# A perceiver layer stack with windowed attention and a quantised feed-forward: the last gated columns rounded on GpSimd, and a new order from the end of the last layer on

## The reference

```python
x = x + xattn(layernorm(x), ctx, seg)   # 4 layers: self-attention, masked cross-attention, gated feed-forward; rmsnorm at the end
x = x + attn(layernorm(x))              # each token looks at the 16 before it: sigmoid(q k / 4) times v, Wo, layernorm
x = x + ffn(layernorm(x))               # quantised
```

```python
_weight_quant(w): scale = 1 / clip(mean(|w|), 1e-5);  clip(round(w * scale), -1, 1) / scale
_act_quant(x):    scale = 127 / clip(max(|x|, -1), 1e-5);  clip(round(x * scale), -128, 127) / scale
_bitlinear(x, w) = _act_quant(x) @ _weight_quant(w).T
out = _bitlinear(silu(_bitlinear(x, w_gate)) * _bitlinear(x, w_up), w_down)
```

## Time and profile before

| | |
|---|---|
| median of 3 runs | 622.28 us (620.0 to 622.4) |
| the profiled execution's own time | 619.67 us |
| its span, first to last instruction | 617.9 us |
| mean granted TensorE clock | 0.991 of full speed |
| busy: PE, DVE, ACT, POOL | 564.1, 353.5, 279.5, 117.7 us |
| split_low, L1903 | 64 instructions, 48.0 us, mean 755 ns |

### The profile page before, as it was taken

The page is one execution under the profiler, slowest core; times in us unless marked ns, Lnnn a source line. Parts: engine busy times, 40 slices in busy tenths (PEclk is TensorE's granted clock), DMA queues, the critical chain, the costliest instruction groups (busy, mean ns, idle before and its releaser), DMA issues.

```text
span 617.9 us, 13676 instructions
## 1 busy us (share of the span) xinstructions
PE 564.1 (91%) x5806; PEld 421.8 (68%) x5806; DVE 353.5 (57%) x680; ACT 279.5 (45%) x490; POOL 117.7 (19%) x124
## 2 busy tenths in 40 slices
PE   4989998999999899999998989999898989999855
PEld 1666655988767566988766658987666558897523
DVE  5896445466564454674554455574554364752787
ACT  0254444633355336433544446342554547445523
POOL 4252100012323100020612000122312001252110
PEclk9999999999999999999999999999999999999969
DMA  8800020010500200201400200204000200000001
GB/s 334 345 2 25 12 69 2 5 65 1 205 2 4 102 1 3 68 1 27 180 1 36 70 2 2 69 1 189 16 2 1 71 0 2 0 1 2 2 1 39
DMA packets 4676, 30.29 MB, mean 49 GB/s; under 512 B 1153, under 2 KB 1665, under 8 KB 2818
## 3 DMA queue, kind: packets, MB, share of 16 engines
q1 hardware_dynamic: 4610, 29.35, 12.5%
HBM read 28.82 MB, written 0.52 MB: 47 GB/s over the span
## 4 chain that ended last, share of the span: by engine, by line
PE 77%; DVE 10%; ACT 8%; issue 3%; POOL 1%; DMA 1%; SPq 0%; DVEq 0%; POOLq 0%
PE psD L326 18%; PE QD L621 12%; PE psD L634 9%; PE QD L408 6%; PE QD L443 4%; ACT PTR L1253 3%; PE psD L320 3%; PE QD L436 3%; PE QD L394 3%; DVE AQ L1803 3%; PE psD L463 2%; PE QD L431 2%; PE psD L359 2%; PE psD L484 2%; PE psD L470 2%
## 5 line engine op out<-in xcount | busy, mean ns | idle before, releaser
L1253 ACT ACTIVATE PTR<-QD 128x2048 f32<-128x2048 f32 x40 | 75.1, 1878 | 41.8 <-PE QD L443 21.5
L326 PE MATMUL psD<-WAB,hT 128*128 128x256 f32 (+1 forms) x216 | 70.1, 465 | 2.2 <-DVE hT L1744 2.2
L2492 POOL TENSOR_TENSOR rstd<-ms,mhalf 128x2 f32<-128x2 f32 x26 | 19.9, 764 | 271.8 <-DVE ms L1729 270.6
L1803 DVE TENSOR_REDUCE AQ<-QD 128x8 f32<-128x2048 f32 (+1 forms) x24 | 55.0, 2290 | 27.0 <-PE QD L408 27.0
L621 PE MATMUL QD<-HH,WFH 128*128 128x256 f32 x224 | 67.4, 301 | 0.4 <-DVE WFL L1903 0.4
L1903 DVE TENSOR_TENSOR WFL<-WC,WFH 128x512 fp32r<-128x512 f32 x64 | 48.0, 755 | 32.2 <-ACT WFH L1297 32.1
L621 PE MATMUL QD<-HL,WFH 128*128 128x256 f32 x224 | 63.3, 283 | 0.0
L621 PE MATMUL QD<-HH,WFL 128*128 128x256 f32 x224 | 63.3, 283 | 0.0
L1800 DVE TENSOR_REDUCE AQ<-QD 128x16 f32<-128x2048 f32 x16 | 36.7, 2293 | 39.9 <-PE QD L408 39.9
L634 PE MATMUL psD<-WC,HID 128*128 128x256 f32 x256 | 58.2, 380 | 0.0
L326 PEld LDWEIGHTS psD<-WAB,hT 128*128 128x128 f32 x216 | 39.7, 195 | 21.0 <-issue 14.2
(11 more groups left out here) (172 smaller groups left out, 1021.2 us busy)
## 6 DMA issues: line engine op xcount, KB each, us to landing
WC<-in_wc SPq DMA_DIRECT2D x4, 3072.0 KB, 10.9
WAB<-in_wa SPq DMA_DIRECT2D x4, 1024.0 KB, 4.9
WAB<-in_wb SPq DMA_DIRECT2D x4, 1024.0 KB, 4.7
WF<-in_wf SPq DMA_DIRECT2D x1, 3072.0 KB, 22.8
bias<-in_bias SPq DMA_DIRECT2D x4, 512.0 KB, 3.4
WAB<-in_wt SPq DMA_DIRECT2D x1, 1024.0 KB, 6.0
X<-in_x SPq DMA_DIRECT2D x2, 256.0 KB, 2.8
out_x<-X SPq DMA_DIRECT2D x4, 128.0 KB, 2.4
```

Source lines behind the costliest of these rows:

```text
L326: mm = pe.matmul(bank(l, use)[:, col:col + n], lhs(k), rhs(k), start=(k == 0), stop=(k == KT - 1))
L1253: nc.scalar.activation(PTR[:, r % 2, :], QD[:, :], ACT.Exp, scale=SCALE).then_inc(t_exp, 1)
L1803: v = dve.tensor_reduce(QKR[b][:, t, 0, h, MAXROW].rearrange("p (s r) -> p r s", r=SG_H), QD[:, :].rearrange("p (r s n) -> p r s n", r=4, ...
```

## The change

The diff has two kinds of edits. First, in the quantised block: `round_hidden` moves from VectorE to GpSimd and only subtracts MAGIC; the upper bound 127 moves into VectorE's copy of the transposed columns (`hidden_T`), which bounded below already; `hidden_scales` signals `gq_scale_set` with the reciprocal and a new semaphore `out_scale_set` with the output scale, for which `output` waits. Second, calls stand in another order on all four engines from the last layer's gate_up(0, 5) on.

```diff
@@ VectorE
 def quantise_scales(t, n, src, which):
     ...
-    done(dve.reciprocal(a[:, t:t + n, 2], a[:, t:t + n, 3]))
+    return dve.reciprocal(a[:, t:t + n, 2], a[:, t:t + n, 3])
 def hidden_scales(t):
     dve.wait_ge(qu_free, 2 * t + 2)
-    quantise_scales(t, 1, GU(t).unsqueeze(1), 1)
-    dve.tensor_scalar(sgu[:, t, 2:3], am2[:, t, 3:4], mw[:, 2:3], None, ALU.mult).then_inc(gq_scale_set, 1)
-def round_hidden(t):
-    dve.wait_ge(gq_scaled, t + 1)
-    dve.tensor_scalar(GQ(t), GU(t), MAGIC, 127.0, ALU.subtract, ALU.min).then_inc(gq_set, 1)
+    quantise_scales(t, 1, GU(t).unsqueeze(1), 1).then_inc(gq_scale_set, 1)
+    dve.tensor_scalar(sgu[:, t, 2:3], am2[:, t, 3:4], mw[:, 2:3], None, ALU.mult).then_inc(out_scale_set, 1)
 def hidden_T(t):
-    dve.tensor_scalar(GQT(t), bank(NL, f"gT{t}")[:, :].bitcast(BF16), -128.0, None, ALU.max)\
+    dve.tensor_scalar(GQT(t), bank(NL, f"gT{t}")[:, :].bitcast(BF16), -128.0, 127.0, ALU.max, ALU.min)\
 def output(t):
-    dve.wait_ge(gq_scale_set, t + 1)
+    dve.wait_ge(out_scale_set, t + 1)
@@ GpSimd
+def round_hidden(t):
+    pool.wait_ge(gq_scaled, t + 1)
+    nc.gpsimd.tensor_scalar(GQ(t), GU(t), MAGIC, None, ALU.subtract).then_inc(gq_set, 1)
```

The order, engine by engine (only what moves; the calls around keep their places):

```diff
@@ TensorE
-sums()  gate_up(0, 5)  out_T(1)  gate_up(0, 6)  out_proj(1)  gate_up(0, 7)
+gate_up(0, 5)  out_T(1)  gate_up(0, 6)  out_proj(1)  sums()  gate_up(0, 7)
-window_qk(0, 1)  window_qk(0, 0)
+window_qk(0, 0)  window_qk(0, 1)
-hidden_T(1)  quantised_down(0)  hidden_T(2)
+quantised_down(0)  hidden_T(1)  hidden_T(2)
@@ GpSimd
-scale_ternary(0)  rsqrt(NL-1, 2, 1)  weigh_last(0)  scale_ternary(1)  rsqrt(NL, 0, 0)  ln_rsqrt(2)  add_beta(0)
-scale_ternary(2)  value_pads()  rsqrt(NL, 0, 1)  weigh_last(1)  ln_rsqrt(3)  add_beta(1)
-ln_rsqrt(4)  ln_rsqrt(6)  ln_rsqrt(5)  ln_rsqrt(7)
+value_pads()  rsqrt(NL-1, 2, 1)  scale_ternary(0)  rsqrt(NL, 0, 0)  weigh_last(0)  ln_rsqrt(2)  weigh_last(1)
+rsqrt(NL, 0, 1)  scale_ternary(1)  scale_ternary(2)  ln_rsqrt(3)  add_beta(1)  add_beta(0)
+ln_rsqrt(4)  ln_rsqrt(6)  round_hidden(0)  ln_rsqrt(5)  ln_rsqrt(7)  round_hidden(1)  round_hidden(2)  round_hidden(3)
@@ ScalarE
-... ternary(0)  squares(NL, 0, 0)  ...  gate(1, 7)  ternary(1)  squares(NL, 0, 1)  sigmoid_table()
-window_q(0)  ternary(2)  window_v(0)  sigmoids(0)  sigmoids(1)  copy_oT  window_q(1)  sigmoids(2)  window_v(1)  sigmoids(3)
-quantised_gates(1, 0)  ternary(3)  scale_hidden(0)  quantised_gates(1, 1)
-quantised_gates(2, 1)  scale_hidden(1)  quantised_gates(3, 0)  quantised_gates(3, 1)
+... squares(NL, 0, 0) behind split_high(12)  ...  gate(1, 7)  sigmoid_table()  squares(NL, 0, 1)
+window_q(0)  sigmoids(0)  window_v(0)  sigmoids(1)  copy_oT  window_q(1)  ternary(0)  sigmoids(2)  window_v(1)
+ternary(1)  ternary(2)  sigmoids(3)
+quantised_gates(1, 0)  scale_hidden(0)  quantised_gates(1, 1)  ternary(3)
+quantised_gates(2, 1)  quantised_gates(3, 0)  quantised_gates(3, 1)  scale_hidden(1)
@@ VectorE
-means() ahead of residual(1)
+means() behind tokens_low(1); split_low(8), (9) and (10) each one or two calls earlier
+layernorm_stats(2) and layernorm_apply(2) ahead of hidden(1, 6)
-layernorm_stats(7)  round_hidden(0)  layernorm_apply(7)  round_tokens(1)  quantised_hidden(1, 1)  rounded_T(1)  hidden_T(0)
-quantised_hidden(3, 1)  round_hidden(1)  hidden_scales(3)  round_hidden(2)  hidden_T(1)  round_hidden(3)  output(0)
+layernorm_stats(7)  quantised_hidden(1, 1)  layernorm_apply(7)  round_tokens(1)  hidden_T(0)  rounded_T(1)
+quantised_hidden(3, 1)  hidden_scales(3)  hidden_T(1)  output(0)
```

More of the change, by code:

```diff
@@ L1102, in rest @@
                 out_proj(NL - 1, 1, "cwo1", Woc, "coT1")
+                sums()
                 gate_up(NL - 1, 0, 7)
@@ L1651, in rest @@
                     all_blocks(NL - 1, 1)
+                gate(NL - 1, 0, 5)
+                copy_oT(NL - 1, 1, "coT1")
+                gate(NL - 1, 0, 6)
                 split_high(NL - 1, 8)
-                copy_oT(NL - 1, 1, "coT1")
                 split_high(NL - 1, 9)
-                gate(NL - 1, 0, 5)
                 squares(NL - 1, 2, 1)
-                gate(NL - 1, 0, 6)
                 split_high(NL - 1, 10)
                 gate(NL - 1, 0, 7)
-                ternary(0)
-                squares(NL, 0, 0)
                 split_high(NL - 1, 11)
@@ L1664, in rest @@
                 split_high(NL - 1, 12)
+                squares(NL, 0, 0)
                 gate(NL - 1, 1, 1)
                 split_high(NL - 1, 13)
+                split_high(NL - 1, 14)
                 gate(NL - 1, 1, 2)
[L1668 removed]
+                split_high(NL - 1, 15)
                 gate(NL - 1, 1, 3)
[L1670 removed]
                 gate(NL - 1, 1, 4)
@@ L1674, in rest @@
                 gate(NL - 1, 1, 7)
-                ternary(1)
+                sigmoid_table()
                 squares(NL, 0, 1)
-                sigmoid_table()
                 window_q(0)
-                ternary(2)
+                sigmoids(0)
                 window_v(0)
-                sigmoids(0)
                 sigmoids(1)
@@ L1684, in rest @@
                 window_q(1)
+                ternary(0)
                 sigmoids(2)
                 window_v(1)
+                ternary(1)
+                ternary(2)
                 sigmoids(3)
@@ L1692, in rest @@
                 quantised_gates(1, 0)
-                ternary(3)
                 scale_hidden(0)
                 quantised_gates(1, 1)
+                ternary(3)
                 quantised_gates(2, 0)
                 quantised_gates(2, 1)
-                scale_hidden(1)
                 quantised_gates(3, 0)
                 quantised_gates(3, 1)
+                scale_hidden(1)
                 scale_hidden(2)
@@ L2000, in round_tokens @@
                 ts = (2 * b, 2 * b + 1)
-                quantise_scales(b * 2, 2, hs[:, 2 * b:2 * b + 2, :], 0)
+                done(quantise_scales(b * 2, 2, hs[:, 2 * b:2 * b + 2, :], 0))
                 for t in ts:
@@ L2448, in rest @@
                 layernorm_stats(7, 1, X0)
-                round_hidden(0)
+                quantised_hidden(1, 1)
                 layernorm_apply(7, 1, X0, hs, done)
                 round_tokens(1)
-                quantised_hidden(1, 1)
+                hidden_T(0)
                 rounded_T(1)
-                hidden_T(0)
                 hidden_scales(1)
@@ L2671, in rest @@
                     all_blocks(NL - 1, 1)
+                value_pads()
+                rsqrt(NL - 1, 2, 1)
                 scale_ternary(0)
-                rsqrt(NL - 1, 2, 1)
+                rsqrt(NL, 0, 0)
                 weigh_last(0)
+                ln_rsqrt(2)
+                weigh_last(1)
+                rsqrt(NL, 0, 1)
                 scale_ternary(1)
-                rsqrt(NL, 0, 0)
-                ln_rsqrt(2)
-                add_beta(0)
                 scale_ternary(2)
-                value_pads()
-                rsqrt(NL, 0, 1)
-                weigh_last(1)
                 ln_rsqrt(3)
                 add_beta(1)
+                add_beta(0)
                 ln_rsqrt(4)
                 ln_rsqrt(6)
+                round_hidden(0)
                 ln_rsqrt(5)
                 ln_rsqrt(7)
+                round_hidden(1)
+                round_hidden(2)
+                round_hidden(3)
             with pool.If(nb < 1):
```

33 lines of the change are left out of this document (15 added, 18 removed).

## The result

| | before | after |
|---|---|---|
| median on the chip that ran both | 621.14 us (4 runs, 619.43 to 622.4) | 628.26 us (4 runs, 628.14 to 628.97) |
| the profiled execution, its span | 619.67, 617.9 us | 628.14, 626.3 us |
| mean granted clock | 0.991 | 0.983 |

What follows compares the result with a forecast made beforehand. TensorE's own order of work was taken to bound 520 to 573 us, the chain through VectorE the quantised end. +1.1 + 0.1 - 1.3 = -0.1 gave 619.6 or, on the median's footing, 622.2; forecast 620.9, range 617.6 to 623.3.

Steps and rivals of the forecast that it cites:

- part 4: Quantised end: with GpSimd roundings of 1.1 us, the last output ends at 613.9 instead of 615.17, 1.3 us less.
- rival B: Quantised end: GpSimd rounds at the rate of its two-input add, 2.54 us each, end 3.6 later, 623.3; chance 0.06.
- Part 3: ScalarE's moved ternary calls cost 0.1 us, bounds 0 and 0.6; GpSimd's rounding(0) is done before ln_rsqrt(5) is wanted.
- The forecast's bound for the last gate: Quantised end: ScalarE's last gate comes at most at 606.0 + s, ahead of its remaining scale_hidden calls.
- rival C: Quantised end: TensorE stays at 1.2 GHz up to the last projections, +3.5 us, 623.0; chance 0.05.
- r: Quantised end: time of one rounding on GpSimd, taken as 1.1 us; the old end is passed at 1.35.
- s: Shift of TensorE from the second batch's window scores on, against the kernel before: +1.1 us, alternatives from -0.6 to +1.6.
- Part 2: GpSimd ahead of the second batch, 550 to 565 us: its scalings hold add_layers(1)'s two VectorE instructions, delaying TensorE by 1.1 us.
- Part 1: Layer's end, 520 to 550 us: moving the scalings away shortens split_low and removes TensorE's gap; gain 0.6, bounds 0 and 0.6.
- The footing: Which level of runs the sum starts from: 619.6 by the profiled execution, 622.2 by the median; the middle, 620.9, was given.
- A: Second batch: add_layers(1)'s pair isn't held or precedes the scaling; s -0.6 to -0.1, whole kernel -1.9 to -1.3; chance 0.27.
- D: Besides A, the clock doesn't fall at the quantised end, which is 1.2 us shorter again: 616.5, -3.1; chance 0.08.

Runs made afterwards that it cites:

- e4: Kernel before with nine GpSimd tensor_scalar instructions added behind all else, one at a time; at 1024 columns subtraction alone 2.78 us, multiply and add 1.12.
- e9: Kernel before with six more GpSimd tensor_scalar forms behind all else; multiply-then-add 1.04 us, addition or multiplication alone as slow as subtraction, other pairs 3.63.
- e5: Changed kernel with the rounding on GpSimd written as times 1.0 plus -MAGIC instead of a subtraction; 621.57 us, ratio 1.0014 to the kernel before.
- e6: e5 with GpSimd's scale_ternary(1) and (2) moved behind ln_rsqrt(3) and add_beta(1); 618.94 us, ratio 0.9977 to the kernel before.
- e10: e5 with 16 transpositions of the identity on TensorE in the idle stretch ahead of window_T(1); 620.79 us, ratio 1.0003 to the kernel before.
- e3: Changed kernel with GpSimd's scale_ternary(1) and (2) moved behind ln_rsqrt(3) and add_beta(1); 623.71 us, ratio 1.0065 to the kernel before.
- e11: e6 with 50 transpositions of the identity on TensorE in the idle stretch ahead of rounded_T(1); 617.91 us, ratio 0.9962 to the kernel before.

## Why the prediction was wrong

**The step that failed is one term of part 4: "Rounding of 128x1024 on GpSimd has no row ... I take 1.1".** It takes 2.77 (four instructions, 2767 to 2777 ns), and the upper bound of 2.5 did not hold it either. The chance of 0.06 for rival B was where the outcome lay, though not for rival B's reason, a second input: the rounding has one input and is slower than the 2.5 all the same. The term was read off the scaling because both are one-input TENSOR_SCALAR instructions; the trace's name for an operation doesn't show its two arithmetic operations, and the scaling is the one pair that is quick (e4, e9). The page of the Trainium skill that bears on it (GPSIMD Engine Reference, Engine selection) calls one-input elementwise work "roughly line-rate" on GpSimd; here it is 1.5 times VectorE's 0.68 in the quick form and 4.1 times in the form used.

What this term did to the end, window_sum(1) to last output, where 24.45 was forecast and 31.16 came:

- the three roundings from 610.91 to 619.15 instead of over 3.6 us: 4.64 more;
- their start 18.92 behind window_sum(1) instead of 18.15: 0.77. The fourth rounding has a hand in this. Part 3 had said that rounding(0) is done before ln_rsqrt(5) is wanted, but it runs to 595.01 and ln_rsqrt(5) starts right behind it, so that the 16 matmuls of gate_up start 11.14 behind window_sum(1), against 10.33 in e5 and e6 with a rounding(0) of 1.04: 0.81. They then took 6.31, at the lower clock up to 608, against 5.95 in e6: 0.36. The forecast's bound for the last gate had 0.39 in hand, by e6, whose roundings start 17.76 behind window_sum(1). For the clock part 4 had set a bound of +0.9 and taken 0;
- from the last rounding to the last output 4.00 instead of 2.7: 1.3. TensorE waited 3.44 and 2.11 us between transpositions and went into its last projections at 1.2 GHz. Here rival C's mechanism came in behind rival B's; they had been priced as alternatives.

Rival B's formula, 610.05 + 3r + s, gives with r = 2.77 and s = 2.36 an end of 620.7; the trace has 623.6, of which 0.66 was there from the start. Of the 2.2 left, 2.07 are the last two points; the rest is that the formula allows 2.95 behind the last rounding, where part 4's own steps have 3.2. That the other terms of part 4 add up to the right end shows in e6: with roundings of 1.04 its scale_hidden(3) starts at 608.48 (608.45 + s was forecast, s being about 0 there) and its last output at 613.40 (613.4).

**Part 2: the mechanism right, the size half** (s, the delay of TensorE at this place, 2.36 instead of 1.1). As forecast, the engines alternated: each of add_layers(1)'s two instructions waited for one scaling, 3.20 for the two against 0.88, and window_T(1) waited 1.99 for hs. The rule that part 4 quotes from the Trainium skill, that the later instruction blocks until the other has finished, speaks for part 2 and not against it, as part 4 has it. The scores started at 564.58, that is 0.91 later than before without the 0.66; 1.1 was forecast. But then TensorE's clock fell, and the scores took 1.91 and 2.06 instead of 1.02 and 1.49: another 1.45 in s, 2.36 in all, in this execution. "All that follows on TensorE is carried along" missed that an idle stretch also slows what comes behind it; the clock had been weighed in part 4 alone. e10 takes that away with the wait left in, and e3 and e6 take the wait away: by the ratios e5 to e6 is 0.37%, or 2.3 us, and e10 to e6 0.26%, or 1.6.

**Part 1: right.** No gap at 539, split_low at 0.69, and the last layer's second down starts at 546.25 against 546.30 although everything ahead was 0.66 late: 0.7 gained, 0.6 forecast. It is used up in part 2.

**Part 3: right on ternary,** 15.87 against 15.85 us between the window_sums, where 0.1 was forecast; wrong on rounding(0), as said above.

**The footing.** The sum was made on 619.6 and given as 620.9, between two levels of the runs. That is small beside the miss. Between the two profiled executions -0.1 was forecast and 8.46 came: 6.7 of the difference are part 4, 1.26 are s, and 0.66 was there before the first changed call.

**The rivals.** A is refuted by the 3.20. D's clock gain did not come by itself. In e11's trace, with the clock held, the last output comes 1.2 us earlier than in e6's; by the medians it is 1.0, with intervals that overlap. The forecast of no change was nearly right for a kernel with one different line (e5, 1.0014).

What stays open: why the other forms are slow, which no trace shows from outside, why the slow rounding holds nothing on VectorE, and what decides in how many executions the clock falls behind an idle stretch of 2 us.

## What to carry to other kernels

Before work is moved to GpSimd, its own instruction, with its own two arithmetic operations, is to be measured there; a row with the same name and another pair can be off by 2.7 times, and a multiplication by 1.0 may be the cheap way to write a subtraction. A GpSimd instruction like the scaling, long and over SBUF, is put where VectorE has copies out of PSUM or nothing, never in front of the two or three short VectorE instructions on which the next matmul waits, since each of those can wait for one whole GpSimd instruction. Whether a given pair of instructions holds each other is read from a trace: the slow rounding held none. Each GpSimd instruction is also placed against GpSimd's own queue, as rounding(0) ahead of ln_rsqrt(5) shows. A wait of 2 us in TensorE's path is priced with the matmuls behind it at 1.2 GHz as its upper end, and where TensorE must wait anyway, idle work on it can keep the clock.

## What the hardware showed that was not expected

- GpSimd's TENSOR_SCALAR over 128 x 1024 of f32: 1.04 us for multiply and add with two constants, 1.12 with a scale from a column, 2.78 for an addition, a multiplication or a subtraction alone, 3.63 for the other pairs tried; 1.49 for a subtraction over 512 columns. The output's type changes none of it.
- The granted clock fell to 1.2 GHz behind an idle stretch of 1.99 us, where TensorE had been busy before and was busy again behind it. The low stretch lasted from under 4 us (after) to nearly 7 us (e5).
- VectorE's instructions with inputs in SBUF waited for GpSimd's scalings one for one (3.20 and 4.05 us for two instead of 0.87 and 0.74), but not for its roundings of 2.78 us, beside which two of them took 0.87.
- Idle transpositions of the identity for 5.62 us held the clock at 1.00 through a stretch that had been low in the kernels before, after and e6.
